# Three edits to one four-layer kernel: attention block order, float32r feed-forward passes, mixing on TensorE

## The chip, the cores and the metric

The kernel runs on one core of one Trainium2 chip. The metric is the device time of one execution in microseconds (us). The core has five engines with queues of their own: TensorE (PE, matrix products; its weight loads are shown as PEld), VectorE (DVE), ScalarE (ACT), GpSimd (POOL) and SyncE (SP, which issues most DMAs).

## The reference, cut to what matters

Twelve steps work on x of shape (4, 512, 128), 2048 tokens. Each adds a sublayer of the layer-normed x to x.

```python
x = x + 0.5 * ffn0(ln(x));  x = x + gated_scan(ln(x));  x = x + 0.5 * ffn0(ln(x))
x = x + 0.5 * experts_top1(ln(x));  x = x + attention16(ln(x));  x = x + 0.5 * experts_top1(ln(x))
x = x + 0.5 * experts_top2(ln(x));  x = x + diff_attention2(ln(x));  x = x + 0.5 * experts_top2(ln(x))
x = x + 0.5 * gated_ffn(ln(x));  x = x + diff_attention3(ln(x));  x = x + 0.5 * gated_ffn(ln(x))

def attention16(x):                     # 16 heads of 8; queries and keys are both x, values are the whole rows
    y = x.reshape(b, t, 16, 8).transpose(0, 2, 1, 3)
    attn = softmax(einsum('bhtk,bhsk->bhts', y, y) / sqrt(8))
    o = einsum('bhts,bsc->bhtc', attn, x)            # 128 columns for each head
    return o.transpose(0, 2, 1, 3).reshape(b, t, 16 * 128) @ weight

def experts_top2(x):                    # 8 experts, 128 -> 512 -> 128, the best two of each token
    probs = softmax(xf @ router_w.T);  topv, topi = top_k(probs, 2);  topv = topv / (topv.sum() + 1e-9)
    return sum over the two choices of topv * (gelu(xf @ w1[e]) @ w2[e])

def gated_ffn(x):                       # 8 experts of width 64, the two best kept, scale s (t, e)
    xs = s.T[:, :, None] * xf[None];  h = silu(xs @ w1) * (xs @ w3);  return sum over e of h @ w2
```

## The kernel before, in words

X holds the 16 tiles of 128 tokens in SBUF, four tiles to a batch b. Each step is one block: every engine has its own program, written out by hand, semaphores order them, and a barrier stands between blocks. PSUM is eight banks of 128x512 f32. There is no planner: an engine does what its program lists, in that order.

**attention1** (the 16-head attention) works through 32 items n; an item is one pair of heads of one batch (eight items to a batch), and its 8 scores i are four key tiles kt for each of the pair's two heads j. On TensorE a score is one bf16 matmul (L2831) into a ring of four banks, so it waits until the exponential four places before it has read its bank (bank_free). ScalarE takes exponentials (L2916, and L2915 for the copy HIGHS). VectorE (L2974) makes LOWS, what HIGHS leaves out. value(n, j) is twelve float32r matmuls of 512 columns (L2842 to L2844) over the four kt: NH by HIGHS, NH by LOWS, NL by HIGHS. gather (L2857) multiplies by the output weight, and join (L2985) adds to X. Scores run one item ahead of values. Once a batch, at the item with n % 8 == AT_SPLIT == 2, the next batch's queries and keys are made: project (L2810, f32, takes a place in the ring) on TensorE, high (L2900) on ScalarE, rest (L2959) on VectorE, mid (L2904) on ScalarE, low (L3036) on POOL, each followed by DMAs to DRAM on SP; the next batch's operands QS and KS come back by DMA. For the very first items a small set of DMAs ("quarter", L2786) loads items 1 to 3's first part.

**moe(2, ...)** (experts_top2; two such stages) sorts (token, choice) pairs into 32 row tiles by expert and runs 39 turns r of (tile, expert). POOL gathers rows by indirect DMA (L1176) and scatters results (L1184). TensorE turns a tile (L1207), does up (L1215) and down (L1229). VectorE copies the turned tile into XR (L1471) and XT (L1482) and adds into Y (y, L1493). At the end SP loads both choices' rows back for each batch (L1162, into YB[0], which is N, and YB[1]). ScalarE scales YB[1] by its gate CW (L1340, four tiles); VectorE scales YB[0] (L1526), adds it to X (L1528) and adds YB[1] (L1532). Then come the moments for the next norm, and, where a step with a router follows, score_ahead on TensorE (turns L369, scores L359 of the next router) with take_ahead on ScalarE (L382). Only where a router follows does TensorE run matmuls whose result is not read ("unread", L1244) before the rows are back; that holds for the second such stage, in front of the feed-forward, and not for the first, in front of diff_attention.

**ffn3** (gated_ffn; two such stages) first works out the routing on VectorE (a chain of small operations up to the cast L1782, with one exponential on ScalarE). Then 16 units u = (b, it), it being one quarter of the 8x64 hidden columns: project (L1640) is two f32 matmuls of 512 columns into two banks; expand (L1659) spreads the scales over 128 rows, ScalarE copies them (CX, L1719), VectorE multiplies (z, L1790, two operations), ScalarE takes silu (L1731), VectorE multiplies (hT, L1798), and from the second batch on down (L1671) and the residual (L1804) follow. project(u) waits for z of unit u - 2. In the first ffn3 the weights are centred first on TensorE (L1678) and copied by ScalarE (L1705).

## Time and profile before

| | us |
|---|---|
| median of 3 runs | 1703.02 (1702.91 to 1708.54) |
| profiled execution, its own time | 1702.36 |
| its span | 1700.5 |
| busy PE | 1432.8 |
| busy DVE | 1198.5 |
| busy ACT | 1111.8 |
| busy POOL | 460.1 |

The profile shows one execution. Times in it count from the start of the span. A matmul in f32 leaves two records, one in float32r or bf16 one. An engine's busy time says nothing on its own on what sets the time, since the twelve blocks follow one another: attention1 lies from about 261 to 580 us, the first moe(2, ...) ends at about 800, the second at about 1332, and the two ffn3 follow at 1332 and at 1636.

### The profile page before, as it was taken

What the parts mean: (1) busy time and instruction counts of PE and PEld (TensorE: products, weight loads), DVE (VectorE), ACT (ScalarE), POOL (GpSimd) and SP (SyncE); (2) the same over time, 40 slices, a digit from 0 to 9 for tenths busy, and PEclk for the clock granted to TensorE, in tenths of its full rate; (3) what the DMA queues carried; (4) which work ended last, traced back from release to release, by engine and by line L of the source; (5) the groups of instructions that cost most, each with busy time, mean ns of one, the idle gap of its engine ahead of it and who ended that gap; (6) DMA issues with size and microseconds to landing.
All of it is one profiled execution on the core that took longest, in us unless ns stands there. A gap on an engine that the chain in (4) does not pass through costs nothing. (4 is left out here: it accounts for less than half of the span.)

```text
span 1700.5 us, 29624 instructions
## 1 busy us (share of the span) xinstructions
PE 1432.8 (84%) x9239; PEld 833.1 (49%) x9239; DVE 1198.5 (70%) x2827; ACT 1111.8 (65%) x2522; POOL 460.1 (27%) x610
## 2 busy tenths in 40 slices
PE   4798668999999695884799999998578887999979
PEld 4355564777777594784222222223477452222255
DVE  6477645877788746325999999995622767999566
ACT  3454556988888573444489898985444444888833
POOL 1231434433433242652130202011364000221100
PEclk8698787999999797987799999999789897999979
DMA  2002214220300243112330304002111204222000
GB/s 83 5 1 100 76 54 119 59 60 16 75 1 1 62 133 112 43 42 75 87 88 1 87 2 107 1 1 103 49 43 61 74 18 129 74 74 62 1 1 25
DMA packets 75077, 93.81 MB, mean 55 GB/s; under 512 B 11200, under 2 KB 61504, under 8 KB 74544
## 3 DMA queue, kind: packets, MB, share of 16 engines
q1 hardware_dynamic: 67088, 77.27, 16.0%
q0 software_dynamic: 6144, 12.60, 2.6%
q10 hardware_dynamic: 1696, 2.10, 0.6%
q8 instruction: 77, 1.26, 0.3%
q14 instruction: 72, 0.59, 0.1%
HBM read 57.22 MB, written 34.70 MB: 54 GB/s over the span
## 5 line engine op out<-in xcount | busy, mean ns | idle before, releaser
L2387 DVE TENSOR_REDUCE MAXI<-psum 128x1 f32<-128x512 f32 x768 | 473.0, 683 | 36.0 <-PE psum L2108 31.8
L2276 ACT ACTIVATE BIG<-psum 128x512 f32<-128x512 f32 x768 | 410.8, 609 | 61.1 <-PE psum L2129 54.6
L2108 PE MATMUL psum<-KM,QS 64*128 64x512 bf16 x768 | 254.5, 401 | 42.0 <-DVE MAXI L2387 25.9
L2129 PE MATMUL psum<-QM,KM 64*128 64x512 bf16 x768 | 233.2, 386 | 2.2 <-DVE REST L2377 1.9
L2139 PE MATMUL psum<-BIG,VST 128*32 128x512 f32 x1536 | 204.6, 604 | 4.9 <-ACT OT L2290 4.2
L2974 DVE TENSOR_TENSOR LOWS<-EX,HIGHS 128x1024 fp32r<-128x1024 f32 x128 | 158.2, 1240 | 61.5 <-POOL HIGHS L3030 31.9
L1215 PE MATMUL psum<-m_XT,m_W 128*128 128x128 f32 x992 | 145.3, 294 | 27.7 <-DVE m_XT L1482 22.6
L2108 PEld LDWEIGHTS psum<-KM,QS 64*128 64x128 bf16 x768 | 56.8, 94 | 223.3 <-DVE MAXI L2387 194.6
L2916 ACT ACTIVATE EX<-psum 128x512 f32<-128x512 f32 x256 | 153.7, 608 | 18.0 <-PE psum L2831 18.0
L3030 POOL CAST HIGHS<-EX 128x512 fp32r<-128x512 f32 x128 | 109.1, 852 | 179.2 <-ACT EX L2916 114.7
L1215 PEld LDWEIGHTS psum<-m_XT,m_W 128*128 128x128 f32 x992 | 132.0, 207 | 36.0 <-DVE m_XT L1482 28.1
L1229 PE MATMUL psum<-BIG,m_H 128*128 x992 | 135.4, 282 | 0.3
L1493 DVE SCALAR_TENSOR_TENSOR m_Y<-psum,m_MASK,m_Y 128x128 f32 x124 | 43.5, 351 | 125.6 <-PE psum L1229 105.4
L2551 POOL CAST NM<-MAXI 128x16 bf16<-128x16 f32 x48 | 12.2, 254 | 428.7 <-DVE MAXI L2387 428.7
L1229 PEld LDWEIGHTS psum<-BIG,m_H 128*128 128x128 f32 x992 | 125.5, 199 | 0.8 <-issue 0.7
L1176 POOL DMA_INDIRECT m_XG<-rows,m_ROWS x96 | 93.1, 970 | 111.2 <-DVE m_ROWS L1417 52.9
L1184 POOL DMA_INDIRECT y<-m_Y,m_ROWS x96 | 93.7, 976 | 79.8 <-DVE m_Y L1493 70.7
L2842 PE MATMUL psum<-HIGHS,NH 128*128 128x512 f32 x256 | 110.0, 430 | 0.0
L1329 ACT ACTIVATE m_H<-psum 128x512 f32<-128x512 f32 x78 | 46.4, 594 | 93.6 <-PE psum L1215 60.5
L1310 ACT ACTIVATE m_W<-BIG 128x512 f32 x124 | 78.6, 634 | 42.0 <-DVE m_PLACE L1431 38.9
L2129 PEld LDWEIGHTS psum<-QM,KM 64*128 64x128 bf16 x768 | 56.9, 93 | 96.0 <-ACT BIG L2276 82.8
L2844 PE MATMUL psum<-HIGHS,NL 128*128 128x512 f32 x256 | 101.6, 397 | 0.0
(363 smaller groups left out, 2557.2 us busy)
## 6 DMA issues: line engine op xcount, KB each, us to landing
BIG<-in_w_dram SPq DMA_DIRECT2D x24, 512.0 KB
parts<-PART SPq DMA_DIRECT2D x24, 384.0 KB, 2.6
parts<-PART SPq DMA_DIRECT2D x24, 256.0 KB, 2.3
rows<-N SPq DMA_DIRECT2D x16, 256.0 KB, 2.7
N<-y SPq DMA_DIRECT2D x16, 256.0 KB, 4.0
QS<-parts SPq DMA_DIRECT2D x32, 128.0 KB, 3.9
QS<-parts SPq DMA_DIRECT2D x14, 256.0 KB, 5.8
parts<-PART SPq DMA_DIRECT2D x24, 128.0 KB, 1.8
```

The source lines that it names most:

```text
L1215: last = pe.matmul(up_banks[r % len(up_banks)][:, it * P:(it + 1) * P], W[:, r % DEEP, it * P:(it + 1) * P], XT[:, r % XS, :], start=True, ...
L1229: last = pe.matmul(down_at(r), H[:, r % HS, it * P:(it + 1) * P], DOWN[:, bass.ds(e, 1), it * P:(it + 1) * P].rearrange("p e n -> p (e n)" ...
L2108: last = pe.matmul(peaks_at(PK * n + i)[:, k, :], QS[r, buf, g, qt * P:(qt + 1) * P], KM[r, buf, g, m, :], start=True, stop=True)
L2129: pe.matmul(bank_of(("score", n, i)), KM[r, buf, g, m, kt * P:(kt + 1) * P], QM[r, n % 2, MAPS[at] // slots, :], start=True, stop=True).th ...
L2139: last = pe.matmul(banks[4][32 * j:32 * j + 32, :], VST[:, n % 2, c, j // 2, :], EX[n % 2][:, c, j, :], start=c == 0 and n % GROUP == 0, s ...
L2276: act.activation(EX[n % 2][:, kt, MAPS[j], :], bank_of(("score", n, i)), ACT.Exp, scale=SM_SCALE).then_inc(S["exp"].sem, 1)
L2387: dve.tensor_reduce(MAXI[:, n % 2, qt, columns], peaks_at(PK * n + i), AX, ALU.max, negate=True).then_inc(S["reduced"].sem, 1)
L2842: pe.matmul(banks[4 + j], NH[:, t, :], HIGHS[:, pair(n, kt), j, :], start=kt == 0, stop=False)
L2844: last = pe.matmul(banks[4 + j], NL[:, t, :], HIGHS[:, pair(n, kt), j, :], start=False, stop=kt == TB - 1)
L2916: act.activation(EX[:, kt, j, :], bank_of(("score", n, i)), ACT.Exp, scale=SM_SCALE, accum_out=SUMS[:, n % 2, j, kt:kt + 1]).then_inc(S["e ...
L2974: dve.tensor_tensor(LOWS[:, pair(n, kt)], EX[:, kt], HIGHS[:, pair(n, kt)], ALU.subtract).then_inc(S["low"].sem, 1)
L3030: pool.tensor_copy(HIGHS[:, pair(n, kt), 0, :], EX[:, kt, 0, :]).then_inc(S["high"].sem, 1)
```

## The change: what it does

- attention1: value(n, 0) now always comes after the next item's first four scores (before, the very first one came ahead of them), and project comes behind value(n, 0) instead of ahead of it. On VectorE rest comes after the second LOWS instead of the first, on ScalarE mid after the eighth exponential instead of the sixth.
- moe(2, ...): during turns 4 to 35 VectorE writes 32 diagonal matrices, the identity times one gate column, into tiles of XR that are read no more. At the end TensorE multiplies them with the rows of both choices and sums in PSUM (banks 4 to 7), and VectorE adds one bank per batch to X. The scalings on ScalarE and VectorE go. Turns and scores of the next router come between the mixes.
- ffn3: from unit 2 on the projection is three float32r passes, high by high, high by low and low by high part, of operands that ScalarE (XH, WH) and VectorE (XL, WL) make before the first unit is scaled.

```diff
@@ moe, TensorE @@
-                self.score_ahead(pe, fresh)
+                if not one:
+                    pe.wait_ge(S["weighed"].sem, S["weighed"].at(1 + M))
+                    for b in range(B):
+                        pe.wait_ge(back[b].sem, back[b].at(16 * K))
+                        for t in range(TB):
+                            for k in range(K):
+                                last = pe.matmul(banks[4 + b][:, t * P:(t + 1) * P], XR[:, k * NT + b * TB + t, :],
+                                                 YB[k][:, b * TB + t, :], start=(k == 0), stop=(k == K - 1))
+                        last.then_inc(S["mixed"].sem, 1)
+                        if b:
+                            self.score_ahead(pe, fresh, [b - 1])
+                    self.score_ahead(pe, fresh, [B - 1])
+                else:
+                    self.score_ahead(pe, fresh)
@@ moe, ScalarE @@
-                if not one:
-                    for b in range(B):
-                        act.wait_ge(back[b].sem, back[b].at(32))
...
-                            last = act.activation(YB[1][:, t, :], YB[1][:, t, :], ACT.Copy, scale=CW[:, 1, t:t + 1])
...
+                for b in range(B):
+                    self.take_ahead(act, b)
@@ moe, VectorE @@
+                def gate(i):
+                    k, t = i // NT, i % NT
+                    if i == 0:
+                        dve.wait_ge(S["weighed"].sem, S["weighed"].at(1))
+                    dve.tensor_scalar(XR[:, i, :], self.ident[:], CW[:, k, t:t + 1], None, ALU.mult
+                                      ).then_inc(S["weighed"].sem, 1)
...
                     y(r, tiles[r])
+                    if not one and E // 2 <= r < E // 2 + M:
+                        gate(r - E // 2)
...
-                    dve.wait_ge(back[b].sem, back[b].at(16 * K))
-                    if not one:
-                        ch.link(dve.tensor_tensor(YB[0][:, t, :], YB[0][:, t, :],
-                                                  CW[:, 0, t].unsqueeze(2).broadcast_to([P, TB, C]), ALU.mult))
-                    ins = dve.tensor_tensor(X[:, t, :], YB[0][:, t, :], X[:, t, :], ALU.add)
-                    if not one:
-                        ch.link(ins)
+                    if one:
+                        dve.wait_ge(back[b].sem, back[b].at(16))
+                        more = YB[0][:, t, :]
+                    else:
                         dve.wait_ge(S["mixed"].sem, S["mixed"].at(b + 1))
-                        ins = dve.tensor_tensor(X[:, t, :], YB[1][:, t, :], X[:, t, :], ALU.add)
-                    ins.then_inc(fresh.sem, 1)
+                        more = banks[4 + b].rearrange("p (t c) -> p t c", t=TB)
+                    dve.tensor_tensor(X[:, t, :], more, X[:, t, :], ALU.add).then_inc(fresh.sem, 1)
@@ ffn3, TensorE @@
+                    if u == 2:
+                        pe.wait_ge(S["low_weights"].sem, S["low_weights"].at(1))
+                    if u == 2 or (b and it == 0):
+                        pe.wait_ge(S["low"].sem, S["low"].at(b + 1))
...
-                        last = pe.matmul(banks[4 + 2 * (u % 2) + s], self.f3w[:, s, it * P:(it + 1) * P],
-                                         nT[:, b * L:(b + 1) * L], start=True, stop=True)
+                        if u < 2:
+                            last = pe.matmul(out, self.f3w[:, s, inner], nT[:, columns_of], start=True, stop=True)
+                            continue
+                        pe.matmul(out, WH[:, s, inner], XH[:, columns_of], start=True, stop=False)
+                        pe.matmul(out, WH[:, s, inner], XL[:, columns_of], start=False, stop=False)
+                        last = pe.matmul(out, WL[:, s, inner], XH[:, columns_of], start=False, stop=True)
@@ ffn3, ScalarE @@
-                act.wait_ge(S["shifted"].sem, S["shifted"].at(1))
-                act.activation(rt[:, 1], rt[:, 0], ACT.Exp).then_inc(S["powered"].sem, 1)
+                for b in range(B):
+                    t = slice(b * L, (b + 1) * L)
+                    act.activation(XH[:, t], nT[:, t], ACT.Copy).then_inc(S["high"].sem, 1)
+                    if b == 1:
+                        act.wait_ge(S["shifted"].sem, S["shifted"].at(1))
+                        act.activation(rt[:, 1], rt[:, 0], ACT.Exp).then_inc(S["powered"].sem, 1)
...
+                act.activation(WH[:], self.f3w[:], ACT.Copy).then_inc(S["high"].sem, 1)
@@ ffn3, VectorE @@
+                def low(b):
+                    t = slice(b * L, (b + 1) * L)
+                    dve.wait_ge(S["high"].sem, S["high"].at(b + 1))
+                    dve.tensor_tensor(XL[:, t], nT[:, t], XH[:, t], ALU.subtract).then_inc(S["low"].sem, 1)
+
                 routed()
+                dve.wait_ge(S["high"].sem, S["high"].at(B + 1))
+                dve.tensor_tensor(WL[:], self.f3w[:], WH[:], ALU.subtract).then_inc(S["low_weights"].sem, 1)
+                for b in range(B):
+                    low(b)
                 scale(0)
@@ attention1, TensorE @@
-                        if n == 0 and j == 0:
-                            value(n, j)
                         for i in range(4 * j, 4 * j + 4):
                             if n + 1 < items:
                                 score(n + 1, i)
+                        value(n, j)
                         u = ("project", (n + 1) // per_b + 1, 0)
                         if j == 0 and u in turn and (n + 1) % per_b == AT_SPLIT:
                             bank_free(u)
                             project(u[1], bank_of(u))
-                        if n or j:
-                            value(n, j)
@@ attention1, ScalarE @@
-                        if u in turn and n % per_b == AT_SPLIT and i == 5:
+                        if u in turn and n % per_b == AT_SPLIT and i == 7:
                             mid(u[1])
@@ attention1, VectorE @@
-                        if u in turn and (n + 1) % per_b == AT_SPLIT and kt == 0:
+                        if u in turn and (n + 1) % per_b == AT_SPLIT and kt == 1:
                             rest(u[1], bank_of(u))
```

## Rows read from the trace of the kernel before

**Rows 1.** The page's first line.
```profile
span 1700.5 us, 29624 instructions
```
**Rows 2.** Windows view of a stretch of attention1; column names stand in its first line.
```profile
core 0: us, PE busy (x) PEld busy (x) DVE busy (x) ACT busy (x) POOL busy (x), PEclk, DMA share, GB/s
320.00:360.00 40.00, 40.00 (x220) 30.76 (x219) 31.54 (x60) 35.51 (x100) 15.58 (x18) 1.00 0.00 1
```
**Rows 3.** Timeline of TensorE in attention1: start, duration, engine, line, operation, releaser in brackets.
```profile
339.40 0.60 PE L2831 MATMUL psum<-QS,KS 48*128 48x512 bf16 x4
...
343.78 0.60 PE L2831 MATMUL psum<-QS,KS 48*128 48x512 bf16 x4
344.31 0.50 PE L2842 MATMUL psum<-HIGHS,NH 128*128 128x512 f32 x1
344.65 0.39 PE L2843 MATMUL psum<-LOWS,NH 128*128 128x512 f32 x1
344.88 0.39 PE L2844 MATMUL psum<-HIGHS,NL 128*128 128x512 f32 x1
```
**Rows 4.** Timeline of attention1 around the third projection.
```profile
434.20 0.60 PE L2831 MATMUL psum<-QS,KS 48*128 48x512 bf16 x4
...
435.44 1.12 PE L2810 MATMUL psum<-nT,ORDER 128*128 128x512 f32 x2 [0.64 <-ACT EX L2916]
...
441.22 0.39 PE L2831 MATMUL psum<-QS,KS 48*128 48x512 bf16 x1 [0.48 <-DVE REST L2959]
...
446.30 0.50 PE L2842 MATMUL psum<-HIGHS,NH 128*128 128x512 f32 x1
```
**Rows 5.** Timelines of the two tails of moe(2, ...) and of what follows the first.
```profile
787.04 1.28 ACT L1340 ACTIVATE m_YB<-m_YB,m_CW 128x128 f32<-128x128 f32 x4 [9.53 <-DMA m_YB<-y]
...
797.04 0.69 DVE L1532 TENSOR_TENSOR X<-m_YB,X 128x512 f32<-128x512 f32 x1
...
802.29 1.97 PE L459 MATMUL psum<-ident,N 128*128 128x128 f32 x8 [22.63 <-DVE N L423]
...
1316.85 1.47 PE L1244 MATMUL psum<-m_OHS,identb 128*128 128x512 bf16 x6 [1.42 <-DMA m_YB<-y]
...
1328.29 3.42 PE L359 MATMUL psum<-centred,nT 128*128 128x8 f32 x16
```
**Rows 6.** Timeline before the second ffn3: the same 16 records.
```profile
1634.01 1.91 PE L359 MATMUL psum<-centred,nT 128*128 128x8 f32 x16
```
**Rows 7.** Timeline of the second ffn3.
```profile
1643.92 0.23 DVE L1782 CAST f3parts<-f3left 128x128 bf16<-128x128 f32 x1
...
1647.36 2.72 DVE L1790 TENSOR_TENSOR f3z<-psum,f3cx 128x512 f32<-128x512 f32 x4 [3.21 <-ACT f3cx L1719]
...
1648.70 3.78 PE L1640 MATMUL psum<-nT,f3w 128*128 128x512 f32 x4 [1.66 <-DVE f3z L1790]
...
1652.79 1.98 PE L1640 MATMUL psum<-nT,f3w 128*128 128x512 f32 x4
...
1655.02 1.99 PE L1640 MATMUL psum<-nT,f3w 128*128 128x512 f32 x4
...
1665.83 1.88 PE L1640 MATMUL psum<-nT,f3w 128*128 128x512 f32 x4
...
1668.96 1.88 PE L1640 MATMUL psum<-nT,f3w 128*128 128x512 f32 x4
...
1689.83 2.94 PE L1671 MATMUL psum<-f3d,f3hT 128*128 128x128 f32 x24
```
**Rows 8.** The page's costliest groups: busy, mean ns, idle time before and releaser.
```profile
L2974 DVE TENSOR_TENSOR LOWS<-EX,HIGHS 128x1024 fp32r<-128x1024 f32 x128 | 158.2, 1240 | 61.5 <-POOL HIGHS L3030 31.9
...
L1493 DVE SCALAR_TENSOR_TENSOR m_Y<-psum,m_MASK,m_Y 128x128 f32 x124 | 43.5, 351 | 125.6 <-PE psum L1229 105.4
```
**Rows 9.** Timeline at the start of attention1: a DMA issue and the second values.
```profile
272.20 0.77 SPq L2786 DMA_DIRECT2D KS<-parts  x2
...
282.30 0.79 PE L2842 MATMUL psum<-HIGHS,NH 128*128 128x512 f32 x1
```
**Rows 10.** Source view of line 1482: duration ns least, median, greatest.
```profile
L1482 DVE COPY m_XT<-m_XR x78: 226/227/440, 682.9 to 1303.6; 128x128 f32 x78
```

27 lines of the change are left out of this document (16 added, 11 removed).

## Prediction

> **What bounds the kernel now.** I read the page first: the profiled execution took 1702.36 us for a span of 1700.5 us, so what is cut out of the span comes off the time one for one [rows 1]. Then, for each of the three places that the diff touches, the timeline. The stages follow one another behind barriers, so each place has a bound of its own.
>
> In the 16-head attention TensorE never rests: 40.00 of 40 us busy [rows 2]. Half an item (four scores, twelve float32r matmuls, a gather) takes 343.78 - 339.40 = 4.38 us, and one float32r pass of 512 columns follows the next after 344.88 - 344.65 = 0.23 us (0.227 over many), the first of a row after 0.34 [rows 3]. Only around a "project" does it stop. The four scores at 434.20 are through by 434.73 (343.78 to 344.31, 0.53 us, in a plain half, [rows 3]), yet the projection starts at 435.44, released by ScalarE's exponentials: 0.71 us idle. Later the eighth score waits for VectorE's REST until 441.22 [rows 4].
>
> At the end of a two-choice expert stage VectorE makes three passes over each batch. The first expert tail starts with data back at 787.04 and its last addition ends at 797.04 + 0.69 = 797.73; the second ends on TensorE, whose last scores end at 1328.29 + 3.42 = 1331.71 [rows 5]. Those 16 records take 3.42 us there and 1.91 us where the clock is full, so the second tail now ends at half clock [rows 5, 6].
>
> In the last feed-forward TensorE sets the pace once the down projections run: one unit takes 1668.96 - 1665.83 = 3.13 us. Before that, a loop of project, expand, copy and two multiplies gives 1655.02 - 1652.79 = 2.23 us a unit [rows 7].
>
> **Attention: the project behind the values.** Nothing is added; the projection, the residue and the middle part move. From 434.20 to the next half's first value record at 446.30 there are 12.10 us [rows 4]; two plain halves and that record's 0.53 us make 9.29 us, and the projection itself, in the size of one f32 pass pair, some 0.86 us. So 12.10 - 9.29 - 0.86 = 1.95 us are stall and type switches. With the values first, the 0.71 us goes. ScalarE can round the projection as soon as it has taken the values, about when TensorE is through the gather, but VectorE now does one more LOWS (1.24 us, [rows 8]) before the residue, so the eighth score still waits about 0.5 us. Putting the middle part after the eighth exponential frees the following scores. I keep 0.75 of the 1.95 us, so 1.2 us go, three times: -3.6 us. The bounds are 0 and 3 x 1.95 = 5.9 us. Behind the moved part on ScalarE are the next item's exponentials (0.6 us later, where TensorE is four scores ahead), and behind POOL's low part the DMAs of the next batch, which have five items, over 40 us, to land.
>
> **Attention: first item.** Now the values (0,0) come ahead of the second item's scores, and the second values start at 282.30 [rows 9]. In the new order four scores come first. They need the quarter whose KS pieces SP issues from 272.20 on, two at once taking 0.77; with a landing of over 2 us behind the issue, TensorE idles to about 275. Then twelve values at 0.43 us (0.23 doubled) end near 281, while ScalarE gets its exponentials early, and the second values start at about 281.5, more of them at full clock. Estimate: 0.8 us from the start and 1.2 us from the clock, -2.0 us. Bounds: +1.5 (the landing is late) and -4.
>
> **Gates.** In each two-choice stage, 32 multiplications of a 128x128 identity by a column are put behind y in turns 4 to 35. The trace has no such instruction; the nearest is the SBUF to SBUF copy of the same size, 0.227 us median, 0.440 at most [rows 10]. Bounds: 0, and 64 x 0.44 = 28 us if all lie on the path. VectorE stands idle 125.6 us before the 124 y's of all expert stages, a mean of 1.0 us a turn [rows 8], which covers a gate; it waits there for TensorE's down projections, and so they hide it. If that cover goes, as where TensorE itself waits for m_XT, a gate costs its length. I take four gates in 64 on the path: +1.0 us.
> The Trainium skill, SBUF — State Buffer, section "Who interferes with whom", speaks against this edit: a tensor_scalar in a two-port mode takes the port pair shared with GpSimd, which then can't write DMA descriptors. By it 64 gates would hold POOL up by up to their own length, and the reverse. The spread of the copy, 0.227 to 0.440, agrees that somebody waits there. What the sum would be by it is that of the rival of the gates below.
>
> **Tails.** Removed: four ScalarE scalings and two of three VectorE passes for each batch. Added: eight f32 matmuls of 128x128 by 128, 16 records. 24 records of this kind take 2.94 us with the drain of the last, about 0.115 each [rows 7], so 1.83 us a batch at full clock, 3.66 at half.
> First tail: TensorE idles 22.6 us before 802.29 and is slow when it returns, eight records in 1.97 us [rows 5]; so I take it as cold at 787.04. Mix 0 ends at 790.7; the clock comes up after about four us of dense work, as it did between 1648.70 (3.78 us for a projection) and 1652.79 (1.98) [rows 7]. Then 1.83 each, part of the second slow: mixes end at 792.8, 794.6, 796.5, and the last addition (0.25 to see it, 0.69) at 797.45 against 797.73: -0.3 us. Bounds: full clock throughout -1.6 us; half clock throughout 787.04 + 14.6 + 0.9 = 802.5, +4.8 us.
> Second tail: TensorE has just run its unread matmuls, from 1316.85 on, six of 0.23 us, to 1318.2 [rows 5], and now goes straight on, so I take full clock. It must do four mixes (7.3), four turns (about 0.45 each, 1.8), four scores (64 records of 0.12, less the waits: 4 x 0.92 = 3.7): 12.8 us, end near 1331.1 against 1331.71, -0.5 us. Half clock: 14.6 + 3 + 7.3 = 25 us, end at 1343, +11.6 us.
>
> **Feed-forward.** From unit 2 on each unit replaces two f32 matmuls (four records; 1.98 us with the drain of the last at 1652.79, 1.72 from start to start as I take it, [rows 7]) by six float32r passes of 0.227 [rows 3], 1.36 us: -0.36 us. TensorE paces ten units: -3.6 us. In four more the project is in a two-unit loop, so half of it counts: -0.7 us. Added ahead: ScalarE rounds four batches and the weights (4 x 0.6 + 1.05 us), VectorE takes WL (1.24 us as LOWS, [rows 8]) and four lows (0.61 each behind one another): 3.7 us. In the second feed-forward VectorE is idle from 1643.92 + 0.23 to 1647.36, 3.2 us [rows 7], which hides all but 0.5 us. The first new project is at half clock there, 6 x 0.43 = 2.6 against 3.45, -0.8 us more. Second: -4.6 us.
> In the first the cover is smaller by some 0.5 us, +1.0. If the centring matmuls come at half clock (two f32 matmuls, like the projection of 3.78 us in [rows 7]), the two roundings ahead of the exponential make it late by 1.3 us; if TensorE comes warm out of the tail, not. With TensorE idle longer before unit 2, it may fall to half clock, up to +2 us. I take +1.9 in all against -4.3: -2.4 us.
>
> **Sum.** -3.6 - 2.0 + 1.0 - 0.3 - 0.5 - 4.6 - 2.4 = -12.4 us. From 1702.36 that is 1690.0; the median of the runs lies 0.66 us above the profiled one, so 1690.5 us.
>
> **Rivals.**
> *TensorE is the new bound of a tail.* The mixes stay cold in the first tail and partly in the second, where scores queue behind them. [...] Price +5 us: 1695.5. The Trainium skill, TensorE: Matmul & The Clock Gate, section "What's actually happening", says that the slow clock is the default and that activity releases it; by it neither tail could stay cold for long under dense mixes.
> *The gates show in part.* Catch-up stretches, where TensorE waits for m_XT, hold a third of them: 21 x 0.35 = 7 us, 1697.
> *More than I count.* Mixes keep the clock up into the next stage, whose first eight records now take 1.97 us, and into the first feed-forward: 5 us more, 1685.5.
> *The other side.* VectorE becomes the bound of the expert loop: every gate lengthens its turn. 64 x 0.25 = 16 us, up to 28: 1706 to 1718. It decides from 0.2 us a gate on the path (64 x 0.2 = 13). Against it: the mean idle of 1.0 us ahead of each y [rows 8].
> *The change does nothing*: the project gains only move a wait to REST and the roundings eat the passes' gain. Then the parts leave -3: 1699.
>
> **How the numbers follow.** Forecast (1686 to 1694.5) 0.56; more than I count 0.12; cold tail 0.13 (half of it still under 1694.5); gates in part 0.09; nothing 0.05; other side 0.05. A change of 0.5% is 8.5 us, about what a measurement of this kernel tells from none: faster means under 1694.5, slower over 1711.5. Faster 0.56 + 0.12 + 0.07 = 0.75; slower 0.02 of the other side, with a little for the unforeseen 0.03; the same 0.22. Range: from the better case, 1684, to beyond the gates in part, 1698.
>
> **What would show it.** In the attention: no wait for EX before a project, a half with a project near 5.3 us, the second values near 281.5. In the tails: 16 records in 1.83 us a batch, or 3.66 if I am wrong about the clock; last addition near 797.5 less the attention's gain. In the loop: VectorE's idle time ahead of y shorter by the gates, and y no later. In the feed-forward: units of 2.77 us instead of 3.13 and 2.05 instead of 2.23, VectorE's first multiplication some 0.5 us later after its last cast. Wrong would be the prediction if the mixes ran cold, if the gates lengthened turns, or if a float32r group cost more between bf16 and f32 ones than 0.1 us.

## The result and the profile after

| | us |
|---|---|
| before, median of 10 runs beside the changed kernel | 1703.93 (1697.93 to 1708.54) |
| changed, median of 10 runs | 1695.24 (1691.32 to 1697.22) |
| ratio | 0.9947, 95% interval 0.9930 to 0.9963 |
| profiled execution, changed | 1692.17, span 1690.4 |
| forecast | 1690.5, range 1684 to 1698 |

The changed kernel is 8.7 us faster by the medians and 10.1 us by the two profiled spans [rows 1]; the forecast was 12.4. A second comparison on another chip (`changed_again`, below) gave 0.9923, 0.9906 to 0.9939, which is 13.1 us of 1707.03. The forecast lies between the two.

The profiled execution of the kernel before is one of its quick ones: 1702.36 us, with a granted clock of 0.907 in the mean, where the kernel before took 1707 to 1710 us beside the later comparisons, with medians of 0.901 to 0.904. The changed kernel's ten runs have a median of 0.910. All readings by place below are taken against that one execution.

The page of the changed kernel begins so (busy time of each engine, its share and its instructions):

```profile
span 1690.4 us, 30028 instructions
PE 1431.6 (85%) x9423; PEld 851.2 (50%) x9423; DVE 1204.6 (71%) x2885; ACT 1109.3 (66%) x2500; POOL 460.9 (27%) x610
```

TensorE lost 1.2 us of busy time and VectorE won 6.1: busy time tells nothing of where 10 us went. The stages do. Each begins with ScalarE's square root for its norm, so the distance from one such root to the next is a stage with its barrier. Worked out from the traces, in us:

```
stage           before  changed  changed_again  only_attention  only_mixing  only_ffn
gated scan      119.32   121.87      121.98         121.03        121.03      120.94
attention1      318.00   313.54      313.28         311.65        318.84      318.78
two-choice, 1   142.05   144.13      143.66         143.62        142.52      142.50
two-choice, 2   144.08   143.44      144.64         144.40        142.92      144.99
ffn3, first      62.00    61.17       60.03          64.30         62.11       60.25
diff_attention3 242.29   239.53      243.13         242.99        242.53      242.35
ffn3, second     64.24    60.08       60.03          63.64         64.27       60.38
```

Two rows without any edit in them (gated scan, diff_attention3) move by up to 3.6 us between executions, and so does the first ffn3 where it has no edit (62.00 us before, 64.30 in `only_attention`). So I compare events inside a stage, and whole stages only where several kernels agree.

**Attention.** TensorE around the third projection, to be set beside [rows 4]:

```profile
431.31 0.60 PE L2875 MATMUL psum<-QS,KS 48*128 48x512 bf16 x4
...
434.71 1.02 PE L2854 MATMUL psum<-nT,ORDER 128*128 128x512 f32 x2
435.56 1.05 PE L2901 MATMUL psum<-WL,OT 128*128 128x128 f32 x8
436.55 0.60 PE L2875 MATMUL psum<-QS,KS 48*128 48x512 bf16 x3
437.46 0.39 PE L2875 MATMUL psum<-QS,KS 48*128 48x512 bf16 x1 [0.31 <-DVE REST L3000]
```

No wait stands ahead of the projection (L2854); the half with it takes 436.55 - 431.31 = 5.24 us; the eighth score waits 0.31 us for REST. From the four scores to the next half's first value there were 12.10 us [rows 4] and are 10.85. Laid over before, the first values record of a half runs 2.87 us ahead from the first projection on, 4.1 from the second, and 5.40 us from the third to the end. How much of it was there ahead of the first projection is less sure than these figures look: `only_mixing` and `only_ffn`, which have the old order of the attention, run 0.84 and 0.77 us behind the kernel before from the fourth half on, and the kernels with both edits of the attention end 4.87 (`mended`) to 6.36 us (`only_attention`) ahead of it. What the second and the third projection add is the same in every one of them, 1.25 to 1.28 us each.

At the start of the stage:

```profile
276.65 1.03 PE L2875 MATMUL psum<-QS,KS 48*128 48x512 bf16 x4 [2.29 <-DMA KS<-parts]
...
282.88 0.50 PE L2886 MATMUL psum<-HIGHS,NH 128*128 128x512 f32 x1
```

TensorE waits for the quarter's DMA as forecast. The stage itself began 1.25 us later in this execution, so the second values come 0.66 us earlier behind its start than in [rows 9].

**Gates and loop.** Groups by line: count, busy time, mean ns, and idle time ahead of the engine with its cause.

```profile
L1494 DVE SCALAR_TENSOR_TENSOR m_Y<-psum,m_MASK,m_Y 128x128 f32 x124 | 43.5, 351 | 126.7 <-PE psum L1229 99.2 <-remote 15.9 <-issue 9.6
...
L1508 DVE TENSOR_SCALAR m_XR<-ident,m_CW 128x128 f32<-128x128 f32 x64 | 18.2, 284 | 0.0
...
L1184 POOL DMA_INDIRECT y<-m_Y,m_ROWS x96 | 93.9, 978 | 81.7 <-DVE m_Y L1494 72.8 <-issue 8.8
```

A gate takes 0.284 us, longer than the copy's median that I took for it. VectorE doesn't idle ahead of it, and it still idles 126.7 us before the y's (125.6 in [rows 8], where the gates' 18.2 should have come off). The time comes off elsewhere. Ahead of the copy into XT, which mostly waits for VectorE's own copy into XR, before and changed:

```profile
L1482 DVE COPY m_XT<-m_XR 128x128 f32 x78 | 20.7, 265 | 30.8 <-DVE m_XR L1471 17.3 <-PE psum L1215 8.8 <-issue 4.7
...
L1483 DVE COPY m_XT<-m_XR 128x128 f32 x78 | 20.3, 260 | 20.9 <-PE psum L1215 7.5 <-DVE m_XR L1472 7.5 <-issue 6.0
```

From a y to the copy into XT behind it there are 0.87 us without a gate, 0.90 with one between them and 1.05 with three (medians, two-choice loops of the kernel before, of the changed one and of `gates_three_times`). So it is this wait that takes up a gate. Turns became longer for another reason in some executions; see the experiments.

**Tails.** First tail: TensorE's first mix, VectorE's first and last addition.

```profile
785.16 0.77 PE L1296 MATMUL psum<-N,m_XR 128*128 128x128 f32 x2 [7.49 <-DMA m_YB<-y]
...
788.95 0.69 DVE L1540 TENSOR_TENSOR X<-psum,X 128x512 f32<-128x512 f32 x1 [10.81 <-PE psum L1296]
...
794.92 0.69 DVE L1540 TENSOR_TENSOR X<-psum,X 128x512 f32<-128x512 f32 x1
```

Mixes start at half clock: two records in 0.43 us (787.00 to 787.43, say), later in 0.22. The granted clock is 0.50 from the first mix to 790.0 and 1.00 behind it, so TensorE worked for 4.9 us at half clock. From the rows' return to the next stage there are 13.30 us against 13.55 before. Second tail:

```profile
1315.44 1.47 PE L1244 MATMUL psum<-m_OHS,identb 128*128 128x512 bf16 x6 [1.76 <-DMA m_YB<-y]
1316.74 0.38 PE L1296 MATMUL psum<-N,m_XR 128*128 128x128 f32 x2
...
1327.37 1.91 PE L359 MATMUL psum<-centred,nT 128*128 128x8 f32 x16
1329.60 3.54 PE L1701 MATMUL psum<-f3w,CENTRE 128*128 128x512 f32 x4 [0.32 <-PEq L1140]
```

Full clock at the first mix and at the last scores (16 records in 1.91 us; 3.42 in [rows 5]), and half clock right behind them, at the centring (granted 1.00 from 1316.0 to 1329.3 and 0.50 from 1329.6 to 1332.7). The tail takes 14.16 us from the rows' return where it took 15.2.

**Feed-forward.** First one: ScalarE's exponential, VectorE's wait for it, VectorE's added work, the first new projection, and the expansions of three units.

```profile
1335.18 0.31 ACT L1734 ACTIVATE rt<-rt 128x128 f32<-128x128 f32 x1
...
1335.59 0.29 DVE L1805 TENSOR_REDUCE rt<-rt 128x16 f32<-128x128 f32 x1 [1.08 <-ACT rt L1734]
...
1338.40 1.22 DVE L1850 TENSOR_TENSOR f3wl<-f3w,f3wh 128x1024 fp32r<-128x1024 f32 x1
1339.54 2.49 DVE L1846 TENSOR_TENSOR f3xl<-nT,f3xh 128x512 fp32r<-128x512 f32 x4
...
1343.28 0.80 PE L1662 MATMUL psum<-f3xh,f3wh 128*128 128x512 f32 x1 [2.81 <-DVE f3z L1822]
1343.88 0.63 PE L1663 MATMUL psum<-f3xl,f3wh 128*128 128x512 f32 x1
...
1352.33 0.39 PE L1682 MATMUL psum<-f3ct,f3selb 24*128 24x512 bf16 x1
...
1354.36 0.38 PE L1682 MATMUL psum<-f3ct,f3selb 24*128 24x512 bf16 x1
...
1357.16 0.38 PE L1682 MATMUL psum<-f3ct,f3selb 24*128 24x512 bf16 x1
```

Units take 2.03 us (2.23 before) and then 2.80 (3.13). What is added ahead is all there as well: VectorE waits 1.08 us for the exponential, 3.6 us go into the low parts (L1850, L1846), 2.81 us in which TensorE idles, and a first new projection at half clock (0.43 us a pass). First z to last X behind the stage's start: 12.36 and 58.54 us here, 10.51 and 59.37 before, so only 0.83 us are left. In the second feed-forward the exponential is not waited for, z comes at 11.37 instead of 11.06, and the last X at 56.82 instead of 60.93: 4.1 us.

### The profile page after: what moved, and what is told of

Its sections match the earlier page's. It is cut to its first block and busy times, and to the rows that moved or that the text cites. A ratio compares the mean times of both kernels' runs of the same rounds, so it can differ in the third digit from the quotient of the medians.

```text
span 1690.4 us, 30028 instructions
## 1 busy us (share of the span) xinstructions
PE 1431.6 (85%) x9423; PEld 851.2 (50%) x9423; DVE 1204.6 (71%) x2885; ACT 1109.3 (66%) x2500; POOL 460.9 (27%) x610
## 3 DMA queue, kind: packets, MB, share of 16 engines
q8 instruction: 79, 1.29, 0.3%
## 5 line engine op out<-in xcount | busy, mean ns | idle before, releaser
L1494 DVE SCALAR_TENSOR_TENSOR m_Y<-psum,m_MASK,m_Y 128x128 f32 x124 | 43.5, 351 | 126.7 <-PE psum L1229 99.2
```

## Experiments

### Each of the three edits alone

`only_attention`, `only_mixing` and `only_ffn` are the kernel before with the lines of the diff that fall into attention1, moe and ffn3. For the first, the core is:

```diff
+                        value(n, j)
                         u = ("project", (n + 1) // per_b + 1, 0)
                         if j == 0 and u in turn and (n + 1) % per_b == AT_SPLIT:
                             bank_free(u)
                             project(u[1], bank_of(u))
-                        if n or j:
-                            value(n, j)
```

> The kernel before with the new order of the attention alone. The prediction's terms: -3.6 us for the three projections behind the values and -2.0 us for the first item, -5.6 us in all, so a time near 1698 where the kernel before takes 1703.9; the comparison of the two profiles gave -5.4 inside the stage. Rival (the gain only moves to another wait and to the next block's start): under 2 us. In the trace: no wait for EX ahead of the projections, the half with the projection 5.2 us instead of about 6.5, and the rest of the kernel as before but for the start of the next block.

> The kernel before with the gate matrices and the mixing on TensorE alone (both two-choice stages). The prediction's terms: +1.0 (gates) - 0.3 - 0.5 (tails) = +0.2 us; the profile of the changed kernel had -0.25 and -1.0 in the tails, and one more turn of the first stage's loop at half clock (+1.8). Theory: the gates are hidden and that turn was the luck of the clock, so -1.3 us, within +-1 us of it. Rival 1: a gate lengthens its turn, +16 us or more. Rival 2: the gates shift the clock's phases in the loop every time, +0.5 to +1 us, with a half-clock turn near y 23 in this trace too.

> The kernel before with the float32r passes of the feed-forward alone. The prediction's terms: -2.4 and -4.6, -7.0 us in all; the comparison of the two profiles gave -0.8 and -4.2, so -5.0. Theory: -5.0 us again, with the first exponential about 1 us late in the first feed-forward and the first new projection at half clock (0.43 us a pass) in both. Rival: the first feed-forward lost only because TensorE came out of the mixing tail in another state of the clock; then it gives -2.4 here and the whole -7.

The kernel before took 1707.08 us on that chip (28 runs).

| | median | ratio, 95% | by ratio, us | by events inside the stages, us |
|---|---|---|---|---|
| only_attention | 1703.14 | 0.9981 (0.9963 to 0.9999) | -3.2 (-6.3 to -0.2) | -6.4 |
| only_mixing | 1702.51 | 0.9979 (0.9963 to 0.9996) | -3.6 (-6.3 to -0.7) | +0.7 loop, -1.4 tails |
| only_ffn | 1698.73 | 0.9953 (0.9936 to 0.9969) | -8.0 (-10.9 to -5.3) | -1.8, -3.9 |

By places the three make -6.4 - 0.7 - 5.6 = -12.7 us, by ratios -14.8. By ratio every part gains, the first two by little more than nothing, and the sums are no smaller than what the whole change gave (8.7 and 13.1 us), so nothing here says that one part undoes another. The sums by place lie at an end of the intervals for the first two parts and inside that of the third; a part of 4 us can't be weighed better than this by whole runs.

One thing that the sum by place leaves out shows in all executions. `only_mixing` ran with a granted clock of 0.9095 in the median; the kernel before beside it had 0.9025 and the other two parts 0.903. Within the 28 runs of the kernel before, an execution with 0.001 more of granted clock is about 1.15 us shorter. So the mixing may give more than its tails show, by TensorE working more in place of waiting; that the clock is the cause of its 3.6 us isn't shown, since no run holds all else equal.

In `only_mixing` the last y stands 121.82 and 121.57 us behind its stage's start, 121.17 and 121.49 before: +0.7 us. VectorE's idle time ahead of the y's is 125.8 us there, as before, and that ahead of the copies into XT 21.8 instead of 30.8. One turn of the changed kernel's first loop ran at half clock; in `only_mixing` it ran at full clock. In the first two-choice stage of `only_attention`, which has no gates at all, it ran at half:

```profile
748.26 1.85 PE L1215 MATMUL psum<-m_XT,m_W 128*128 128x128 f32 x8 [2.33 <-DVE m_XT L1482]
749.90 1.91 PE L1229 MATMUL psum<-BIG,m_H 128*128 x8
...
752.78 1.06 PE L1229 MATMUL psum<-BIG,m_H 128*128 x8
```

1.91 us for the down projection of one turn, 1.06 for that of the next. Over all 14 profiles the distance from the 23rd y of the loop to the 25th is 5.6 to 5.8 us instead of 4.2 in 9 of 28 stages: 1 of the 6 of kernels without gates, 8 of the 22 with them. The gates don't make it; whether they make it more frequent these counts can't say. Each time it costs 1.4 to 1.6 us, which is most of the 2.2 us by which the last y of the changed kernel's first loop came later. Other stretches at half clock needn't cost anything: the kernel before has three of 3.4 us in its first loop, the last one ending 90 us behind the stage's start, and its last y is the earliest of all.

In `only_ffn` the centring also runs at half clock, but so does most of the projection of units 0 and 1, and then the clock is up where the changed kernel's is down:

```profile
1333.93 3.75 PE L1694 MATMUL psum<-f3w,CENTRE 128*128 128x512 f32 x4 [0.32 <-PEq L1140]
1338.86 5.77 PE L1653 MATMUL psum<-nT,f3w 128*128 128x512 f32 x8 [1.18 <-ACT f3w L1721]
...
1348.09 0.50 PE L1655 MATMUL psum<-f3xh,f3wh 128*128 128x512 f32 x1 [1.60 <-DVE f3z L1815]
1348.43 0.39 PE L1656 MATMUL psum<-f3xl,f3wh 128*128 128x512 f32 x1
```

5.77 us for the eight records (3.70 in the changed kernel), but passes at 0.23 us from the first. So the first feed-forward gives 1.8 us here and 0.8 there: my rival, that its loss depends on the state of the clock in which TensorE comes to it, is right in kind, and the -2.4 that it named is not reached.

Both figures are taken against an execution whose projections ran at full clock (3.70 us). `only_attention` has no edit in this stage, and its projections ran at half clock as those of `only_ffn` did:

```profile
1334.90 5.74 PE L1640 MATMUL psum<-nT,f3w 128*128 128x512 f32 x8 [1.17 <-ACT f3w L1705]
```

Its first z starts 12.81 us behind the stage's start and its last X at 61.67; in `only_ffn` they are at 12.84 and 57.62. With the clock alike at half, the edit gives 4.05 us in this stage and nothing is lost ahead of the first z, since the columns (the parts' matmuls) start at 10.6 us in both, behind the slow projections; with the projections at full clock (before and changed kernel) it gives 0.83.

### Are the gates hidden?

```diff
+                    for q in range(2):
+                        dve.tensor_scalar(MORE[:, (2 * i + q) % 4, :], self.ident[:], CW[:, k, t:t + 1], None, ALU.mult)
                     dve.tensor_scalar(XR[:, i, :], self.ident[:], CW[:, k, t:t + 1], None, ALU.mult
                                       ).then_inc(S["weighed"].sem, 1)
```

> The changed kernel with two more products of the identity and the gate column beside each gate, written to a buffer that nobody reads: 128 more VectorE instructions of 0.28 us in turns 4 to 35. Theory (hidden behind VectorE's idle 1.0 us a turn): turns with TensorE at full clock keep 1.8 us and the kernel is at most 5 us slower than the changed one (1696 to 1700), most of it in turns that catch up after a stop. Rival (VectorE bounds the loop, or GpSimd's indirect DMAs are held up by the shared port): each of the 128 costs its 0.28 us or more, +36 us, a time of 1731 or above; by the port alone the indirect DMAs would be longer than the 978 ns that they take in the changed kernel. The Trainium skill, SBUF - State Buffer, section Who interferes with whom, speaks for this second way.

1692.56 us, ratio 0.9917 (0.9896 to 0.9938). Groups by line of this kernel:

```profile
L1495 DVE SCALAR_TENSOR_TENSOR m_Y<-psum,m_MASK,m_Y 128x128 f32 x124 | 43.4, 350 | 113.1 <-PE psum L1230 95.7 <-remote 14.0 <-DVE m_Y L1495 2.0
...
L1510 DVE TENSOR_SCALAR m_MORE<-ident,m_CW 128x128 f32<-128x128 f32 x128 | 30.5, 281 | 0.0
...
L1185 POOL DMA_INDIRECT y<-m_Y,m_ROWS x96 | 93.7, 976 | 80.1 <-DVE m_Y L1495 71.0 <-issue 9.1
```

48.6 us of VectorE work lie in two loops, and the last y comes 121.79 and 121.75 us behind the start: 0.9 us more than before in both together, with 192 products instead of none. VectorE's idle time pays for it: ahead of all y's 113.1 us instead of 125.6, ahead of the copies into XT 11.3 instead of 30.8. The indirect DMAs take 976 ns, as with 64 gates and before; so the port that the prediction weighed costs nothing here.

### The clock in the first tail

```diff
-                if self.routes:
+                if self.routes or not one:
                     unread(3, 12)
```

> The changed kernel with the unread matmuls also ahead of the first two-choice stage's mixes, where the changed kernel has none. Theory (the first tail's mixes start at half clock because TensorE stood idle): mixes at 0.11 us a record from the first, the first addition 1.7 us after the rows are back instead of 3.8, and from the rows' return to the next block 11.5 instead of 13.3 us, -1.8 us. Rival (the rows' return of the later batches, or VectorE's additions and moments, bound the tail): the first addition comes earlier, but the last only by 0.5 us or less.

```profile
785.39 1.47 PE L1244 MATMUL psum<-m_OHS,identb 128*128 128x512 bf16 x6 [1.30 <-DMA m_YB<-y]
...
788.68 0.69 DVE L1540 TENSOR_TENSOR X<-psum,X 128x512 f32<-128x512 f32 x1 [9.82 <-PE psum L1296]
...
794.04 0.69 DVE L1540 TENSOR_TENSOR X<-psum,X 128x512 f32<-128x512 f32 x1
```

All mixes at 0.11 us a record, yet the first addition starts 3.29 us behind the rows' return (3.79 in the changed kernel), not 1.7: I had left out that the last six unread matmuls stand ahead of the mixes, 1.3 us. The last addition comes 8.65 us behind the return instead of 9.76, so the tail gives 1.1 us, between theory and rival. From the last y to the next stage 19.15 us, against 20.75 and 20.48 in the two profiles of the changed kernel. As a whole 1695.84, ratio 0.9923 (0.9898 to 0.9947), like the changed kernel.

### What the first feed-forward loses

```diff
+                act.wait_ge(S["shifted"].sem, S["shifted"].at(1))
+                act.activation(rt[:, 1], rt[:, 0], ACT.Exp).then_inc(S["powered"].sem, 1)
                 if not kept:
                     for s in range(2):
                         act.wait_ge(centre.sem, centre.at(2))
...
                     act.activation(XH[:, t], nT[:, t], ACT.Copy).then_inc(S["high"].sem, 1)
-                    if b == 1:
-                        act.wait_ge(S["shifted"].sem, S["shifted"].at(1))
-                        act.activation(rt[:, 1], rt[:, 0], ACT.Exp).then_inc(S["powered"].sem, 1)
```

> The changed kernel with ScalarE's exponential of the last feed-forward's routing ahead of the copies of the weights and of all roundings. Theory (in the first feed-forward the two roundings ahead of the exponential cost VectorE its 1.08 us wait): that wait goes, the last cast of the parts comes about 7.6 us after the stage's start instead of 8.67, the first z about 11.3 instead of 12.36, -1.0 us in the first feed-forward and 0 in the second, where the exponential was not waited for. Rival (TensorE's two projections, which follow the centred weights, bound the columns anyway): the columns move by 0.5 us at most and the first z no more than that.

```profile
1338.20 5.84 PE L1660 MATMUL psum<-nT,f3w 128*128 128x512 f32 x8 [1.18 <-ACT f3w L1730]
1343.97 1.06 PE L1669 MATMUL psum<-identb,f3parts 128*24 128x128 bf16 x16
...
1346.16 2.12 DVE L1821 TENSOR_TENSOR f3z<-psum,f3cx 128x512 f32<-128x512 f32 x3 [1.34 <-ACT f3cx L1750]
```

VectorE's wait is gone and the last cast of the parts comes 7.62 us behind the start, as before the change. But here the projections ran at half clock (5.84 us), the columns had to wait for them, and the first z came at 12.91 us, later than in the changed kernel. The new passes then ran at full clock at once and the last X came at 57.67 instead of 58.54. The stage took 60.30 us; that of `changed_again`, where the centring itself ran at full clock (1.95 us) and the exponential, 4.0 us behind the start, was early enough without the edit, 60.03. So the rival holds in this execution: the projections bound the columns. The late exponential is real, it costs at most its 1.08 us, and only when the centring is at half clock; at which clock centring and projections run decides about as much. Ratio 0.9905 (0.9879 to 0.9932), the lowest of the study, but from four runs.

`low_on_gpsimd` also hands the low parts to GpSimd:

```diff
+                for b in range(B):
+                    t = slice(b * L, (b + 1) * L)
+                    pool.wait_ge(S["high"].sem, S["high"].at(b + 1))
+                    pool.tensor_tensor(XL[:, t], nT[:, t], XH[:, t], ALU.subtract).then_inc(S["low"].sem, 1)
@@ VectorE @@
-                for b in range(B):
-                    low(b)
                 scale(0)
```

> As the kernel before it (exponential first), and the four low parts of the activations are made by GpSimd instead of VectorE. Theory (what VectorE has ahead of its first multiplication is a cost on the path): VectorE's 2.49 us of low parts go and the first z starts when ScalarE has spread the scales, about 10.5 us after the start of the first feed-forward (12.36 in the changed kernel) and 11.0 in the second (11.37); units as before at 2.02 and 2.8 us. Together with the exponential -1.9 and -0.4 us against the changed kernel. Rival (both engines share a port): GpSimd's subtractions, 1.2 to 1.7 us each elsewhere in this kernel, or VectorE's routing chain of 0.29 us operations get longer while they run side by side, and the first z comes no earlier than 11.4; the Trainium skill, SBUF - State Buffer, section Who interferes with whom, names tensor_tensor of one engine and the other's as such a pair.

1703.95 us, ratio 0.9974 (0.9957 to 0.9990), slower than `exponential_first` and `warm_first_tail` on the same chip (0.9905 and 0.9923). GpSimd's four subtractions and VectorE's routing chain beside them, in the first feed-forward:

```profile
1334.38 0.29 DVE L1782 TENSOR_TENSOR rt<-rt 128x128 f32<-128x128 f32 x1
1334.39 5.19 POOL L1646 TENSOR_TENSOR f3xl<-nT,f3xh 128x512 fp32r<-128x512 f32 x4 [3.72 <-ACT f3xh L1737]
1334.70 1.25 DVE L1806 TENSOR_TENSOR rt<-rt 128x128 f32<-128x128 f32 x1
1335.98 0.29 DVE L1808 TENSOR_REDUCE rt<-rt 128x16 f32<-128x128 f32 x1
...
1337.16 1.29 DVE L1811 TENSOR_TENSOR rt<-rt 128x128 f32<-128x128 f32 x1
...
1341.54 0.23 DVE L1817 CAST f3parts<-f3left 128x128 bf16<-128x128 f32 x1
```

VectorE's subtraction or product of two SBUF operands takes 0.29 us alone and 1.24 to 1.29 while GpSimd works, as long as one of GpSimd's (5.19 us for four); a reduction keeps its 0.29. The last cast came 11.47 us behind the start instead of 7.62, and both feed-forwards took more (62.60 and 63.30 us). The rival holds. By the Trainium skill, SBUF — State Buffer, section "Who interferes with whom", a VectorE instruction with two inputs in SBUF contends with a GpSimd one that reads SBUF, and tensor_reduce never does; the trace agrees, 1.25 against 0.29 us. The first z, expected at 10.5 us, came at 13.9.

### Warm-up ahead of the units

```diff
+                if kept:
+                    for _ in range(4):
+                        pe.matmul(banks[3], self.f3w[:, 0, 0:P], nT[:, 0:L], start=True, stop=True)
                 pe.wait_ge(S["parts"].sem, S["parts"].at(1))
```

> As the kernel before it (exponential first, low parts on GpSimd), and in the second feed-forward four f32 matmuls of 512 columns whose result nobody reads fill TensorE's 4.3 us of idle time between the second projection and the columns. Theory (the first units of the second feed-forward run at half clock because TensorE stood idle there): the columns run at 0.06 instead of 0.12 us each (-0.8 us), project(2) passes at 0.23 instead of 0.43 us, so -1.2 us more and -2 us in all in the second feed-forward, nothing in the first. Rival (the idle time behind the expansions, 1.9 us, is enough for the clock to fall): columns at full clock but project(2) at 0.43, only -0.8 us or less, since ScalarE's takes follow.

1703.96 us, ratio 0.9963 (0.9946 to 0.9981), and nothing about the clock was learned: GpSimd's subtractions delayed the parts so far that 3.93 us of idle time stood behind the unread matmuls all the same, and columns and first passes ran at half clock. The next kernel has this warm-up without them.

`mended` puts together the exponential first, the unread matmuls in both tails ahead of the rows' return and none behind it, this warm-up, and the low parts in other places:

```diff
-                for b in range(B):
-                    low(b)
+                low(0)
                 scale(0)
                 for u in range(U):
                     if u + 1 < U:
                         scale(u + 1)
                     hidden(u)
+                    if u == 0:
+                        low(1)
+                        low(2)
+                    if u == IT:
+                        low(3)
```

> The changed kernel with four edits at the places where its trace shows a loss: the exponential first; in both mixing tails the unread matmuls ahead of the rows' return (22 of them) but none behind it; VectorE's low parts of the second and third batch behind the first unit's last multiplication and that of the fourth behind the fifth's; in the second feed-forward four unread f32 matmuls between the projections and the columns. Theory, against the changed kernel: first tail -2.3 us (last addition 7.3 us behind the rows' return, not 9.8), second tail -1.3 (first mix at once), first feed-forward -1 to -1.7, second -0.45 (first z at 10.9 behind the stage's start, not 11.4) and -1.2 (units 2 and 3 at full clock): -6 to -7 us in all. Rival: the waits for the rows (up to 3 us) are long enough for the clock to fall without the last six unread matmuls, mixes of the first batch at 0.21 us a record in both tails, then -3 us in all; and the idle time behind the expansions keeps the first new units at half clock whatever comes earlier.

1693.31 us, ratio 0.9919 (0.9901 to 0.9936). TensorE where the second tail's second mix begins, and in the second feed-forward:

```profile
1320.20 0.49 PE L1294 MATMUL psum<-N,m_XR 128*128 128x128 f32 x2 [0.78 <-DMA m_YB<-y]
...
1637.58 3.60 PE L1706 MATMUL psum<-nT,f3w 128*128 128x512 f32 x8
1642.00 1.06 PE L1667 MATMUL psum<-identb,f3parts 128*24 128x128 bf16 x16 [0.83 <-DVE f3parts L1814]
...
1645.54 0.50 PE L1660 MATMUL psum<-f3xh,f3wh 128*128 128x512 f32 x1 [1.60 <-DVE f3z L1822]
...
1646.34 0.51 PE L1660 MATMUL psum<-f3xh,f3wh 128*128 128x512 f32 x1
1646.65 0.63 PE L1661 MATMUL psum<-f3xl,f3wh 128*128 128x512 f32 x1
```

The columns run at full clock (1.06 us; 1.88 in the changed kernel) and the first z comes 10.15 us behind the start instead of 11.37. The first passes run at full clock too, and then, in the middle of the second group, the granted clock falls to half for 3.4 us: the theory holds for four passes, the rival for the next six. The stage takes 58.68 us instead of 60.0, the first feed-forward 59.49. First tail: the last addition starts at 796.36, 8.5 us behind the first mix, which the rows' return released at 787.86 (9.76 in the changed kernel). Second tail: nothing, since the rows of the next batch now bound it (the 0.78 us ahead of 1320.20); what the unread matmuls gave up, the DMA took.

The same edit takes the unread matmuls from the one-choice stages as well, and the second of these took 86.66 us, where the changed kernel's took 83.60 and 84.60. `mended_2` gives them back:

```diff
-                if not one:
+                if self.routes or not one:
                     unread(3, 12)
...
+                if self.routes and one:
+                    pe.wait_ge(back[0].sem, back[0].at(16 * K))
+                    unread(3, 6)
```

> As mended, with the six unread matmuls behind the rows' return put back in the one-choice stages, which mended had lost too (its second one-choice stage took 86.7 us where the changed kernel takes 83.6 to 84.6). Theory: that stage returns to 84.6 us, and the gains seen at their places in mended stay: first tail -1.2 us (19.2 us from the last y to the next stage instead of 20.5 to 20.7), second tail 0, first feed-forward -0.5 to -1, second -1.4 (58.7 us instead of 60.0), so -3 us against the changed kernel, and about -16 us or a ratio of 0.990 against the kernel before. Rival: the places gain and the kernel does not, since what varies from one execution to the next (stages with turns at half clock, 1.6 us each) follows TensorE's load: ratio 0.992 or above.

> The changed kernel itself, as a control on the chip of this comparison. Theory: -8 to -14 us against the kernel before, since three kernels with it inside (gates three times, exponential first, warm first tail) came out at -13 to -16 us on other chips; the turn of the first expert loop at half clock (y 23) is luck and need not return. Rival: the turn at half clock returns, so it belongs to the three edits together.

| | median | before beside it | ratio, 95% | ffn3, first and second | last y to next stage, 1st tail |
|---|---|---|---|---|---|
| changed_again | 1693.95 | 1707.03 | 0.9923 (0.9906 to 0.9939) | 60.03, 60.03 | 20.48 |
| mended | 1693.31 | 1707.03 | 0.9919 (0.9901 to 0.9936) | 59.49, 58.68 | 19.18 |
| mended_2 | 1696.89 | 1710.20 | 0.9916 (0.9895 to 0.9937) | 59.48, 58.73 | 19.25 |

The stage of one choice is back at 84.35 us. The gains at their places repeat to 0.1 us in both mended kernels, some 3.2 us against `changed_again` (1.3 in the first tail, 0.55 and 1.35 in the feed-forwards), about half of what I expected of `mended` and what I expected of `mended_2`; but the ratios don't part from the control's (0.9916 for `mended_2`, between the 0.990 of the theory and the 0.992 of its rival), and the second two-choice stage of `mended_2` took 146.36 us, with a turn at half clock and more. So a kernel that beats both was built by the sum of its places only; as a whole run it is not shown to beat the changed one. And the turn at half clock returned in both stages of `changed_again` (1.4 and 1.6 us), is in none of `mended`, and was in `only_attention`: it is not tied to the three edits.

### The first item of the attention

```diff
                     for j in range(slots):
+                        if n == 0 and j == 0:
+                            value(n, j)
                         for i in range(4 * j, 4 * j + 4):
                             if n + 1 < items:
                                 score(n + 1, i)
-                        value(n, j)
+                        if n or j:
+                            value(n, j)
```

> The changed kernel with the first item of the attention in the old order (the values of its first head ahead of the second item's scores), so that the attention holds the moved projection alone. The prediction gave the first item -2.0 us and the projections -3.6. The attention's stage took 318.0 us before and 313.3 to 313.6 in five kernels with both edits. Theory: the three projections give 3 x 1.25 = 3.8 us and the first item the rest, so the stage takes about 314.3 us here. Rival (the first item's start is where most is gained, and the first projection's gain hides in it): 315.5 or more.

The stage took 314.45 us in a single execution. Event by event it is clearer: the first values record of each half runs 1.02 us ahead of before from the first projection on, 2.3 from the second, 3.56 from the third to the end. The changed kernel's run 5.40 ahead, so the first item gives 1.84 us. Up to the first values the granted clock falls and rises at the same places behind the stage's start in the three executions, to 0.2 us, so they can be set beside one another. (From stage lengths the first item seemed to give 1.1; the rest is lost or won at the barrier behind.)

## Why the prediction was right, by its own steps

- **Attention, projections: -3.6 us forecast, -3.56 measured** (1.02 + 1.27 + 1.27, `old_first_item`). The 0.71 us wait for the exponentials is gone, the half with the projection takes 5.24 us (5.3 said), and the eighth score still waits for REST, 0.31 us at the third projection where I said about 0.5. The 1.02 of the first projection is the unsure one: executions with the same attention differ by 0.8 us up to there. 3.8 us, three times 1.27, is as good a reading.
- **First item: -2.0 forecast, -1.84 measured.** Of it 0.66 us are there at the second values (0.8 said); the rest comes in the halves behind them. The same 0.8 us of spread lies on this term; that both terms fit to 0.2 us is in part luck.
- **Gates: +1.0 forecast, +0.7 measured** (`only_mixing`), +0.9 with three times as many. That VectorE's idle time hides them is right; which idle time is not. I took that ahead of y for the cover and "VectorE's idle time ahead of y shorter by the gates" for the sign of it: 126.7 us instead of some 107 in the changed kernel, 125.8 in `only_mixing`, which has no turn at half clock there. What got shorter is the wait ahead of the copy into XT (30.8 us before, 20.9 and 21.8), and a gate between y and that copy moves it by 0.03 us. Only with three times the gates did the idle time ahead of y shrink as well, to 113.1. The other side, each gate lengthening its turn, would have cost 54 us there (192 by 0.28) and did not; the port held up no DMA (978 and 976 ns, 976 before).
- **First tail: -0.3 forecast, -0.25 measured.** Cold at the start, as said; the clock came up 4.9 us behind the first mix where the working took about four. At the start of the attention in the kernel before, TensorE worked from 271.03 on and had half the clock until 277.0. So the four us are what one row showed and not a rule. With the clock up from the start (`warm_first_tail`) it gives 1.1 us more, so the bound of -1.6 was a fair one.
- **Second tail: -0.5 forecast, -1.0 measured.** The mechanism, full clock through mixes and scores, is right; the size was too cautious: the last scores end at 1329.28, 13.84 us behind the rows' return, where 14.2 were forecast and 14.86 stood before.
- **Second feed-forward: -4.6 forecast, -4.1 measured** (-4.2 and -3.9 in two others). Units of 2.80 and 2.03 us (2.77 and 2.05 said), first z 0.31 us later (0.5 said).
- **First feed-forward: -2.4 forecast, -0.8 measured in the changed kernel, -1.8 in `only_ffn`, -2.0 in `changed_again`.** This is the mis-sized term. I named its three losses (cover, late exponential, clock before unit 2) and counted 1.9 of up to 4.3 us; in the profiled execution all three came in full: parts 1.05 us late, first z 1.85 us late, first passes at 0.43 us. It isn't one number: it is 0.83 us with the projections at full clock and 4.05 with them at half in both kernels (`only_ffn` against `only_attention`), and the forecast of 2.4 lies between the two.

The measured terms make -3.56 - 1.84 + 0.7 - 0.25 - 1.0 - 4.1 - 0.8 = -10.85 us, and the spans differ by 10.1; the remaining 0.75 is what is left of larger parts of both signs: +1.6 us in the two loops beyond the 0.7 counted (the turn at half clock), +0.9 between the attention's last values and its ends, and stages without an edit, of which one moved by +2.6, another by -2.8 and the rest by -1.9 us together, and some 0.3 in the other terms. That the sum comes so near is luck; what the experiments carry are the terms.

The rival "more than I count" saw the clock of the second tail's scores rightly; that it stays up for the feed-forward is wrong in the profiled execution and right in four of the eleven kernels with the mixing, `changed_again` among them, whose centring took 1.95 us. "Cold tails" is right for half of the first tail. "Gates in part" and "the change does nothing" are refuted.

What stays open: why the clock falls in one execution and not in another of the same code, how much of the whole gain is the higher granted clock of the kernels with the mixing, and whether the mended kernel's 3 us are there in the mean.

## What to carry to other kernels

Lay events of a stage over each other from the stage's own start: edits worth 1 us were plain there to 0.1 us where the clock was alike, while whole stages without an edit moved by 3 us and whole runs by 10. Set executions beside one another whose clock is alike at that place: the same edit read as 0.8 or 4.05 us in one stage. Count what a cheaper matmul asks of the other engines before the loop begins, and in which order these engines take it: three passes saved 0.2 to 0.3 us a unit, and with the projections at full clock the first feed-forward had lost 1.85 us before its first multiplication. And VectorE's idle time in a loop that another engine paces really was free: it took 192 more instructions at a cost of 0.9 us. Look where they take it from, though: here it was first a short wait for VectorE's own copy and not the long one for TensorE.

## What the runs showed of the hardware

- A VectorE operation of 128x128 on two SBUF operands takes 0.29 us, and 1.24 to 1.29 while GpSimd subtracts 128x512 (`low_on_gpsimd`); a reduction of the same size is untouched. Moving 2.5 us of work to the idle GpSimd cost 3.9 us on VectorE's chain.
- TensorE's clock can fall to half while it works: behind 16 records of 8 columns that followed one another, with TensorE at work since 1315.44 (the centring at 1329.60), and in `mended` in the middle of a row of float32r passes (from 0.23 to 0.43 us at 1646.5), 1 us after an idle time of 1.60 us had ended. The same code ran its centring in 3.54 us in one execution and in 1.95 in another.
- A transfer bounded what a warm clock could give: in `mended`, without the six unread matmuls the second tail's first batch was mixed at once, and TensorE then waited 0.78 us for the rows of the second.
